# The routing step of an attention and mixture-of-experts kernel: a threshold search by two bits a round, shared between VectorE and ScalarE

## The reference, cut to what matters

```python
logits = xn @ router_weight.T + router_bias          # 8192 x 16
probs = softmax(logits, axis=-1)
_, idx = top_k(logits.T, 512)                        # each expert: its 512 highest tokens
xe = xn[idx]
...
gates = take_along_axis(probs.T, idx, axis=1)
output = zeros.at[flat_idx].add(y * gates[:, :, None])
gate_sums = zeros.at[flat_idx].add(gates)
output = where(gate_sums > 0, output / gate_sums, output)
```

## Time and profile before

| what | value |
|---|---|
| median of 3 runs | 2134.36 us (2132.34 to 2135.39) |
| the profiled execution, its own time | 2125.87 us |
| its span, first to last instruction | 2123.8 us |
| TensorE busy in the span | 1877.1 us (88%) |
| VectorE, ScalarE, GpSimd busy | 1576.4, 1283.8, 1235.5 us |
| route, from its first instruction to the first one of experts | 519.5 to 642.7 us of the span |

### The profile page before, as it was taken

How to read it: one execution, slowest core, us unless ns; L and a number is a source line. 1 busy time by engine, 2 the same in 40 slices (tenths; PEclk the granted TensorE clock), 3 DMA queues, 4 the chain that set the end, 5 groups by cost and what they waited for, 6 DMA issues and landing times.

```text
span 2123.8 us, 41496 instructions
## 1 busy us (share of the span) xinstructions
PE 1877.1 (88%) x12292; PEld 1664.5 (78%) x12292; DVE 1576.4 (74%) x2345; ACT 1283.8 (60%) x2553; POOL 1235.5 (58%) x1203
## 2 busy tenths in 40 slices
PE   1789999986213999999999999999999999999996
PEld 1677888874113888999989989998889988988896
DVE  5778888883784777777778777777777778777763
ACT  3656766762002676766767667676676766766663
POOL 1567777763005556747557585575756758556561
PEclk9899999997555999999999999999999999999998
DMA  5765344433703343425345253442534435244341
GB/s 199 227 190 160 110 114 126 121 83 119 237 7 87 124 107 127 136 97 144 102 131 139 94 144 104 129 137 97 144 95 138 127 107 144 88 144 112 123 126 30
DMA packets 96021, 264.04 MB, mean 124 GB/s; under 512 B 20354, under 2 KB 22114, under 8 KB 93026
## 3 DMA queue, kind: packets, MB, share of 16 engines
q1 hardware_dynamic: 78914, 228.74, 34.1%
q0 software_dynamic: 17056, 34.72, 8.4%
HBM read 224.03 MB, written 56.12 MB: 132 GB/s over the span
## 4 chain that ended last, share of the span: by engine, by line
PE 60%; DVE 2%; POOL 2%; issue 2%; DMA 1%; ACT 1%; DVEq 0%; ACTq 0%; POOLq 0%; SPq 0%
PE experts_b_a L1969 16%; PE experts_b_y L270 10%; PE experts_b_y L271 10%; PE experts_b_y L272 10%; PE experts_b_b L1969 8%; PE experts_b_c L1969 4%; PE experts_b_turn L1949 2%; POOL experts_rows L1632 1%; DVE experts_x_lo L1838 1%; DMA experts_w_raw<-in_w 1%; PE experts_b_turn L1958 1%; PE experts_b_c L1958 1%; POOL experts_s_raw L1604 0%; POOL experts_rows_meta L1617 0%; DVE experts_w_lo L1889 0%
## 5 line engine op out<-in xcount | busy, mean ns | idle before, releaser
L1601 POOL TENSOR_TENSOR experts_s_raw<-experts_w_raw 128x256 f32<-128x256 f32 x128 | 147.1, 1150 | 546.7 <-DMA experts_w_raw<-in_w 545.8
L270 PE MATMUL experts_b_y<-experts_w_hi,experts_h_hi 128*128 128x512 f32 x1024 | 406.7, 397 | 0.0
L271 PE MATMUL experts_b_y<-experts_w_lo,experts_h_hi 128*128 128x512 f32 x1024 | 403.7, 394 | 0.0
L272 PE MATMUL experts_b_y<-experts_w_hi,experts_h_lo 128*128 128x512 f32 x1024 | 398.6, 389 | 0.0
L1969 PE MATMUL experts_b_a<-experts_x_hi,experts_w_hi 128*128 (+1 forms) x1024 | 290.4, 284 | 9.0 <-DVE experts_x_lo L1832 4.1
L1969 PE MATMUL experts_b_a<-experts_x_hi,experts_w_lo 128*128 (+1 forms) x1024 | 290.0, 283 | 0.0
L1969 PE MATMUL experts_b_a<-experts_x_lo,experts_w_hi 128*128 (+1 forms) x1024 | 289.7, 283 | 0.0
L272 PEld LDWEIGHTS experts_b_y<-experts_w_hi,experts_h_lo 128*128 128x128 f32 x1024 | 192.4, 188 | 43.5
L1969 PEld LDWEIGHTS experts_b_a<-experts_x_hi,experts_w_hi 128*128 128x128 f32 x1024 | 194.6, 190 | 30.0 <-issue 5.6
L270 PEld LDWEIGHTS experts_b_y<-experts_w_hi,experts_h_hi 128*128 128x128 f32 x1024 | 194.3, 190 | 23.6
L271 PEld LDWEIGHTS experts_b_y<-experts_w_lo,experts_h_hi 128*128 128x128 f32 x1024 | 194.4, 190 | 20.9
(11 more groups left out here) (320 smaller groups left out, 5454.4 us busy)
## 6 DMA issues: line engine op xcount, KB each, us to landing
experts_w_raw<-in_w SPq DMA_DIRECT2D x256, 512.0 KB, 3.5
attend_bias<-in_bias SPq DMA_DIRECT2D x68, 256.0 KB, 4.0
attend_spread_w<-weight_dram SPq DMA_DIRECT2D x34, 512.0 KB, 6.6
xn_dram<-g_out_row SPq DMA_DIRECT2D x6, 2304.0 KB, 9.5
attend_q_x<-in_x SPq DMA_DIRECT2D x17, 256.0 KB, 3.0
attend_k_x<-in_x SPq DMA_DIRECT2D x17, 256.0 KB, 5.9
xn_dram<-attend_xn SPq DMA_DIRECT2D x17, 256.0 KB, 4.1
experts_b_sb<-in_b SPq DMA_DIRECT2D x16, 256.0 KB, 4.5
```

The lines of the kernel that those rows point to most:

```text
L270: nc.tensor.matmul(out, lh, rh, start=first, stop=False)
L271: nc.tensor.matmul(out, lh, rl, start=False, stop=False)
L272: return nc.tensor.matmul(out, ll, rh, start=False, stop=last)
L1601: nc.gpsimd.tensor_tensor(s1, a21, a22, ALU.add).then_inc(s_done, 1)
```

## The change

Attention: a new step `logits_elsewhere` in the last-but-three edge turn adds the stand-in to the logits of unreached tiles while attention drains, and the four instructions L1350 to L1353 become two copies.

Search: the bits of each logit become a whole number that sorts as the logit does. Its upper 16 bits are searched in eight rounds, then its lower 16 bits in eight more, two bits a round. A round holds three thresholds. VectorE counts against one over 1024 columns and against the third over 384 columns; ScalarE counts against one over 1024 columns and against the third over the other 640, by the sum of signs. Two matmuls add both engines' counts, and two VectorE instructions form the next thresholds. Rounds are written out, without loops.

Softmax: shift, sum, reciprocal and normalising are cut into pieces (`beside`), one behind VectorE's counts of a round; ScalarE's exponential stands behind its counts of the seventh round. Behind the search, greater and equal ones are ranked apart, each by a prefix sum of its own.

```diff
@@ attend, VectorE
+                def logits_elsewhere(n):
+                    done(dve, logits_kept, n)
+                    spare = bias[:, 0:NT * E // P, :].rearrange("p h j -> p (h j)").rearrange("p (t e) -> p t e", e=E)
+                    nc.vector.tensor_tensor(spare, keep["logits"][:, NONE, :].unsqueeze(1).to_broadcast([P, NT, E]),
+                                            spread(keep["unseen"][:, :], [P, NT, E]), ALU.mult).then_inc(elsewhere, 1)
+                    dve.wait_ge(elsewhere, 2)
+                    nc.vector.tensor_tensor(keep["logits"][:, 0:NT, :], keep["logits"][:, 0:NT, :], spare, ALU.add)\
+                        .then_inc(elsewhere, 1)
+                    dve.wait_ge(elsewhere, 3)
...
                     if on(-7):
                         keep_logits(j - 7)
+                    if edge and not on(-3) and on(-4):
+                        logits_elsewhere(j - 7)
@@ route, TensorE
-                with pe.Fori(0, BITS + 1) as i:
-                    pe.wait_ge(counted, i + 1)
-                    nc.tensor.matmul(b_cnt[:, 0:1], same[:, :], count[:, :], start=True, stop=True).then_inc(summed, 1)
+                for r in range(ROUNDS):
+                    pe.wait_ge(counted_a, 2 * (r + 1))
+                    nc.tensor.matmul(b_met[:, 0:4], same_h[:, :], count_a[:, :], start=True, stop=False)
+                    pe.wait_ge(counted_d, 2 * (r + 1))
+                    nc.tensor.matmul(b_met[:, 0:4], same_r[:, :], count_d[:, :], start=False, stop=True).then_inc(summed, 1)
@@ route, ScalarE
-                nc.scalar.activation(gate[:, :, :, :], gate[:, :, :, :], ACT.Exp).then_inc(exp_ready, 1)
+                for r in range(ROUNDS):
+                    act.wait_ge(limit_ready, r + 1)
+                    for k, cols, out in ((1, slice(0, W), slice(0, W)), (3, slice(CUT, W), slice(W, 2 * W - CUT))):
+                        nc.scalar.activation(reached_a[:, out], searched(r)[:, cols], ACT.Sign, bias=limits(r)[:, k:k + 1],
+                                             scale=-1.0, accum_out=count_a[:, k:k + 1]).then_inc(counted_a, 1)
+                    if r == 1:
+                        nc.scalar.activation(low[:, :], low_bits, ACT.Copy, scale=UNIT).then_inc(low_ready, 1)
+                    elif r == 6:
+                        act.wait_ge(shifted, 4)
+                        nc.scalar.activation(gate[:, :, :], gate[:, :, :], ACT.Exp).then_inc(exp_ready, 1)
@@ route, VectorE
+                def search(r):
+                    last_hi, last_lo = r == HALVES - 1, r == ROUNDS - 1
+                    now, data = limits(r), searched(r)
+                    dve.wait_ge(limit_ready, r + 1)
+                    for k, cols, out in ((2, slice(0, W), slice(0, W)), (3, slice(0, CUT), slice(W, W + CUT))):
+                        nc.vector.tensor_scalar(reached_d[:, out], data[:, cols], now[:, k:k + 1], None, ALU.is_ge, ALU.add,
+                                                accum_out=count_d[:, k:k + 1]).then_inc(counted_d, 1)
...
+                        nc.vector.tensor_scalar(next_limit[:, :], ladder[:, :], step_of(r + 1), now[:, 0:1],
+                                                ALU.mult, ALU.add).then_inc(next_ready, 1)
+                    if r in beside:
+                        task, *which = beside[r]
+                        task(*which)
+                    dve.wait_ge(summed, r + 1)
+                    nc.vector.scalar_tensor_tensor(met[:, :], b_met[:, 0:4], 0.0, bound[:, :], ALU.add, ALU.is_ge,
+                                                   accum_out=steps[:, :]).then_inc(met_ready, 1)
...
+                        nc.vector.scalar_tensor_tensor(now[:, :], steps[:, :].to_broadcast([P, 4]), step_of(r),
+                                                       next_limit[:, :], ALU.mult, ALU.add).then_inc(limit_ready, 1)
...
+                for a in range(2):
+                    js = slice(a * J // 2, (a + 1) * J // 2)
+                    nc.vector.tensor_copy(lg[:, js, :, :], by_row[:, js, :, :]).then_inc(lg_ready, 1)
...
+                for a in range(2):
+                    cols = slice(a * HW, (a + 1) * HW)
+                    dve.wait_ge(val_ready, a + 1)
+                    step.step(nc.vector.tensor_scalar(mirror[:, cols], val[:, cols].bitcast(I32), 31, 0x7FFFFFFF,
+                                                      ALU.arith_shift_right, ALU.bitwise_and))
+                    nc.vector.tensor_tensor(key[:, cols], mirror[:, cols], val[:, cols].bitcast(I32), ALU.bitwise_xor)\
+                        .then_inc(key_ready, 1)
...
+                for r in range(HALVES):
+                    search(r)
+                dve.wait_ge(low_ready, 1)
+                nc.vector.scalar_tensor_tensor(rest[:, :], high, found[0][:, :], low[:, :], ALU.subtract, ALU.add)\
+                    .then_inc(limit_ready, 1)
+                for r in range(HALVES, ROUNDS):
+                    search(r)
+                edge = found[1]
+                step.step(nc.vector.tensor_scalar(greater[:, :], rest[:, :], edge[:, :], None, ALU.is_gt))
+                nc.vector.tensor_tensor_scan(rank_g[:, :], greater[:, :], zero[:, :], 0.0, ALU.add, ALU.add)\
+                    .then_inc(gt_ranked, 1)
+                step.step(nc.vector.tensor_scalar(equal[:, :], rest[:, :], edge[:, :], None, ALU.is_equal))
+                nc.vector.tensor_tensor_scan(rank_e[:, :], equal[:, :], zero[:, :], 0.0, ALU.add, ALU.add)\
+                    .then_inc(eq_ranked, 1)
                 dve.wait_ge(gt_summed, 1)
+                step.inc(nc.vector.scalar_tensor_tensor(flag[:, :], rank_g[:, :], b_gt[:, 0:1], greater[:, :],
+                                                        ALU.add, ALU.mult))
                 dve.wait_ge(eq_summed, 1)
+                step.step(nc.vector.scalar_tensor_tensor(place_e[:, :], rank_e[:, :], b_eq[:, 0:1], equal[:, :],
+                                                         ALU.add, ALU.mult))
+                for a in range(2):
+                    cols = slice(a * HW, (a + 1) * HW)
+                    nc.vector.tensor_tensor(flag[:, cols], flag[:, cols], place_e[:, cols], ALU.add).then_inc(pos_ready, 1)
...
+                    held = gate[:, tiles(a, 2), :].rearrange("p t e -> p (t e)")
+                    step.inc(nc.vector.scalar_tensor_tensor(held, b_pos[a][:, :], 0.0, held, ALU.is_lt, ALU.mult))
...
-                step.step(nc.vector.tensor_tensor(gate[:, :, :, :], gate[:, :, :, :], taken[:, :, :, :], ALU.mult))
```

More of the change, by code:

```diff
@@ L1226, in route @@
     W = J * P
+    HW = W // 2
+    ROUNDS = 16
+    HALVES = ROUNDS // 2
+    CUT = 384
+    UNIT = 2.0 ** -16
     with ExitStack() as scope:
+        scope.enter_context(nc.allow_low_precision(reason="counts are whole numbers up to 1024"))
         def sb(name, shape, dt=F32):
@@ L1322, in _ @@
-                pe.wait_ge(gt_counted, 1)
-                nc.tensor.matmul(b_gt[:, 0:1], same[:, :], count[:, :], start=True, stop=True).then_inc(gt_summed, 1)
-                pe.wait_ge(before_ready, 1)
-                pe.wait_ge(eq_counted, 1)
-                nc.tensor.matmul(b_eq[:, 0:1], before[:, :], rank[:, W - 1:W], start=True, stop=True).then_inc(eq_summed, 1)
-                pe.wait_ge(sel_counted, 1)
-                nc.tensor.matmul(b_sel[:, 0:1], before[:, :], rank[:, W - 1:W], start=True, stop=True).then_inc(sel_summed, 1)
@@ new lines, in _ @@
+                pe.wait_ge(before_ready, 1)
+                pe.wait_ge(iota_ready, 8)
+                nc.tensor.matmul(b_gt[:, 0:1], same[:, :], share[:, :], start=True, stop=False)
+                nc.tensor.matmul(b_eq[:, 0:1], same[:, :], share[:, :], start=True, stop=False)
+                pe.wait_ge(gt_ranked, 1)
+                nc.tensor.matmul(b_gt[:, 0:1], before[:, :], rank_g[:, W - 1:W], start=False, stop=True).then_inc(gt_summed, 1)
+                nc.tensor.matmul(b_eq[:, 0:1], same[:, :], rank_g[:, W - 1:W], start=False, stop=False)
@@ L1330, in _ @@
+                pe.wait_ge(eq_ranked, 1)
+                nc.tensor.matmul(b_eq[:, 0:1], before[:, :], rank_e[:, W - 1:W], start=False, stop=True).then_inc(eq_summed, 1)
                 for j in range(J):
+                    if j % 4 == 0:
+                        pe.wait_ge(pos_ready, j // 4 + 1)
                     last = nc.tensor.transpose(b_pos[j // 4][:, (j % 4) * P:(j % 4 + 1) * P],
                                                flag[:, j * P:(j + 1) * P], keep["ident"][:, :])
-                last.then_inc(pos_turned, 1)
+                    if j % 4 == 3:
+                        last.then_inc(pos_turned, 1)
@@ new lines, in total, with invert, normalise @@
+                def total(a):
+                    dve.wait_ge(exp_ready, 1)
+                    t = tiles(a, 2)
+                    soft.inc(nc.vector.tensor_reduce(row_sum[:, t], gate[:, t, :], AX_X, ALU.add))
+                def invert():
+                    soft.wait()
```

(37 more changed lines are left out.)

198 lines of the change are left out of this document (101 added, 97 removed).

## The result

| | before | after |
|---|---|---|
| median, runs side by side | 2133.35 us (2128.02 to 2135.39, 4 runs) | 2098.76 us (2097.36 to 2106.12, 4 runs) |
| ratio | 1 | 0.9849, 95% interval 0.9819 to 0.9878 |
| profiled execution, its own time | 2125.87 us | 2106.12 us |
| its span | 2123.8 us | 2104.4 us |

The change takes 34.6 us off (26 to 39 by the interval); 35.4 were forecast. The profiled execution of after is the slowest of its four runs, and that of before was faster than all four of its own, so their spans differ by 19.4 us only. The sum must therefore be checked stage by stage.

What follows compares the result with a forecast made beforehand. The prediction took one chain, the search, as the bound, with no engine full. Search -27.4, head -2.6, tail -7.1 and attention's end +1.7 sum to -35.4 us, from 2134.4 to 2099.0 us; range 2090 to 2114.

Steps and rivals of the forecast that it cites:

- What bounds it: In route, no engine is full and the search is one chain; whatever leaves it ahead of the gates' write saves time.
- Search, -27.4: Search: sixteen rounds of 3.37 us, ScalarE last by 0.22, plus one 1.32 pass: 55.2 against 82.6 us, 27.4 saved.
- The bound that named 16-bit operands at every second place as unknown: Search: no row showed such operands; VectorE deciding saves another 3.5 us, a ScalarE pass a quarter dearer loses 8.
- Cover: Search rounds: VectorE's small tasks and ScalarE's exponential cost nothing; rival that cover is lost: +8 us, 2107, chance 0.2.
- Head, -2.6: Route's start up to the first count: the count starts at 524.0 instead of 526.6, 2.6 us saved, between 1.5 and 3.
- Tail, -7.1: From search end to gates' reduction: 13.6 us instead of 20.75, 7.1 saved, 6 to 8.
- Attention's end, +1.7: Attention's drain: added step ahead of the out parts delays the projection, 1.7 us lost, 0 to 2.6, more if TensorE's clock falls.
- Slower rival: Search: written-out rounds' instruction fetch stalls VectorE until the input copy lands, 48.8 us on top, 2148; chance 0.04.
- Table rival: ScalarE in the search: sign and exponential in different tables force switches, 2101 to 2103 us; chance 0.08.
- Better than forecast: Search and attention: ScalarE's side as short as VectorE's and attention's step half hidden, 2095 us; chance 0.07.

Runs made afterwards that it cites:

- e4: Changed kernel with the softmax pieces, tile rows and exponential taken out of the rounds and run behind the search; 2103.74 us (1 run).
- e6: Changed kernel with the third threshold split 512 to 512 columns instead of 384 to 640; 2102.86 us (1 run).
- e8: The changed kernel unaltered, run once more on the chip of its neighbours; 2101.93 us (6 runs), ratio to before 0.9838.
- e2: Changed kernel with all GpSimd constants but the first made only once the keys are ready; 2094.32 us (1 run).
- e1: Changed kernel with attention's added step one place later, behind the out parts; 2087.88 us (1 run).
- e7: Changed kernel with the added step later, GpSimd's constants later and the third threshold split evenly; 2093.32 us (5 runs), ratio to before 0.9806.
- e9: The combined kernel e7 with GpSimd's fills placed to run only beside counts; 2091.87 us (4 runs), ratio to before 0.9819.

## Why the prediction was right

The time came out 0.2 us from the forecast, and that closeness is luck. The terms erred both ways: the search and the tail 2.7 us better, the head 2.35 and attention's end 1.9 worse, 1.6 worse in sum by the stages; and the median of before lay 1.0 us lower in these runs than the one that the forecast started from.

- **What bounds it**: right. The chain was the bound, and what came off it came off the time. The end is unchanged at 12.80 us.
- **Search, -27.4**: the mechanism was right, the size was off; it gave -30.0. ScalarE is last, and the two passes were right to 0.01 us (1.15 and 0.81 for 1.14 and 0.82). The term mis-sized is what follows the counts: the sum took 0.62 us for the 0.72 copied from the old matmul of two passes, comparison 0.27 for 0.30, thresholds 0.20 for 0.25. That is 0.18 a round, less 0.01 for the counts: 2.7 us over sixteen. The bound that named 16-bit operands at every second place as unknown was not needed: ScalarE and VectorE take 1.15 and 1.28 us for 1024 of them, and the same for fp32 in the last eight rounds.
- **Cover**: right, by e4.
- **Head, -2.6**: the step that failed is "VectorE meanwhile has the mask and some fifteen small instructions of 0.1 to 0.2 us, done about then". Two of them took 1.08 and 1.79 us beside GpSimd's fills. Before the change they stood behind three passes of 1.23 us and came to run at 523.34, when the fills were over; the change's short copies moved them forward, into the fills. That was the effect to look for: a step brought forward meets other company. With the fills moved the head gives 2.5.
- **Tail, -7.1**: right, -7.18, with the durations of the working. The second place (L1524), two-tensor with two fp32 sources in SBUF, took 1.28 us, as the row of before said. Against the 1.22 us of a one-source reduction the halved rate of the Trainium skill's "Vector Engine (DVE) Microarchitecture Reference", "Points that are easy to get wrong", is again not seen. But a one-source `tensor_scalar` over as many columns took 0.75 us (L1514), and no row compares this form with bf16 sources, so the rule is not refuted either.
- **Attention's end, +1.7**: the mechanism was right, the size was off; it cost +3.6. The 1.7 are there. To them come 0.96 because the out parts were pushed beside GpSimd's product, and 0.84 because TensorE was slower in the projection: 12 matmuls of 0.63 us or more at a granted clock of 0.50, the 1.2 GHz level, against 9 of 0.52 to 0.63 before, ahead of those that come 0.23 us apart, at a granted clock of 1.0, the 2.4 GHz level. The first two parts are in every trace with the step in this place, where the projection starts 5.11 or 5.12 us behind the logits. The third is not shown to be the step's: over these seven traces the projection took 7.04 to 8.11 us, the shortest (e6) less than the 7.24 of before. In the windows the granted clock of the drain was 0.69 before (494.82 to 519.51) and is 0.62 after (0.68 in e8, where the drain is 28.07 us):

```profile
501.97:530.26 28.29, 14.36 (x56) 11.91 (x56) 7.77 (x13) 4.57 (x9) 6.48 (x12) 0.62 0.05 20
```

Here the prediction had named the clock as what could make it more, without a price; its top of 2.6 was too low.
- **Slower rival**: no. The copy lands 53.5 us after its issue at 530.2, and all counts start 3.20 us apart on either side of that, but for the first round (3.27) and the one with the pass between the halves (4.52). **Table rival**: no. Up to experts the trace has one table load (at 0.84 us), as before, and the exponential starts behind its counts without another. **Better than forecast**: not by the way named; ScalarE's counts took what was forecast, and attention's step was not hidden.

## What to carry to other kernels

When a chain is made shorter, look at the small work that stood beside it under cover: its durations were measured where nobody waited for it, and what stretches it where it now runs (here another engine's fills) is the next bound. For a search by counts, share one threshold's columns over two engines first and take more bits a round second, and cut by the end of the slower engine's read, not by columns. A step added to a draining pipeline belongs behind the instructions that feed TensorE: ahead of them it held TensorE up by 2.8 us here, its own length less what there was to spare, plus what the others then ran beside; behind them, by nothing.

## What was not expected of the hardware

**VectorE stops for GpSimd, in some forms.** Beside a GpSimd fill an instruction of plain `tensor_scalar` form over 128 columns took 1.08 and 1.79 us instead of 0.21 and 0.23, one over 4 columns 1.34 instead of 0.23, each ending with the fill. Two-source instructions (L766, L919) stopped for GpSimd's product: the first of the pair of L766 starts 0.21 us behind it, and the pair ends at 506.93, 1.15 behind the product's end at 505.78, where alone it takes 1.28; so nearly all of its work came after the product. Counts with an accumulated result did not stop. The Trainium skill says so in "SBUF — State Buffer", "Who interferes with whom": the two engines share one port pair as an exclusive lock, held for a whole instruction; `tensor_scalar`, copy and cast can take it, unless they write out the accumulator, and two-SBUF-input forms meet only GpSimd's reads. The trace agrees in every one of these cases, and in the kernel before, too, where two-source instructions ran beside the fills in the usual time (timeline of before). The page lets those forms take the pair in certain modes of VectorE only, and which mode it was in, no row here shows. The two instructions add 2.4 us to VectorE's part of the head (1.08 + 1.79 less 0.21 + 0.23), of which e2 shows 2.25 on the path.

```profile
521.04 1.80 POOL L1304 MEMSET route_meta<- 128x2048 f32 x1
522.20 1.23 DVE L1353 TENSOR_TENSOR route_lg<-route_lg,route_stand_in 128x1024 f32<-128x1024 f32 x1
...
523.34 0.22 DVE L1355 TENSOR_SCALAR route_same_i<-route_same_i 128x128 int32<-128x128 int32 x1
523.59 0.23 DVE L1356 TENSOR_SCALAR route_same<-route_same_i 128x128 f32<-128x128 int32 x1
```

**A gap of 0.36 us that stays open.** In some kernels VectorE is idle 0.47 us between the comparison and the thresholds, where it is otherwise 0.11: in the first round of e1, e4, e7 (0.52) and e9, and in the fifteenth of e4. After and its repeat have it nowhere, and the instructions of these rounds are the same. It is of the size of the jump back's 0.37, which makes the fetching of code a candidate; that was not tested, and it is worth at most 0.7 us here.
